# Operand places and a four-product last score tile in a fused attention and feed-forward block

## The reference

```python
xn = layernorm(x)                                   # no weights
q, k, v = (gelu(xn @ W1 + b1) @ W2 + b2 for each)   # 256 -> 256 -> 256
scores = tril(q @ k.T) / sqrt(256 * 512)            # a mask of zeros, no softmax
s = layernorm(scores @ v) * ln_w + ln_b
W = clip(round(W / (mean(abs(W)) + EPS)), -1, 1)    # for both feed-forward weights
g = silu(relu(xn @ W1q.T + b1) @ W2q.T + b2)        # 256 -> 1024 -> 256
out = x + s * g
```

## Time and profile before

| | before |
|---|---|
| median of 3 runs | 309.36 us (308.67 to 310.17) |
| the profiled execution | 308.97 us, its span 307.2 us |
| granted TensorE clock, mean | 0.998 of full speed |
| TensorE matmul busy | 301.1 us (98%) |
| VectorE busy | 246.6 us (80%) |
| ScalarE busy | 221.2 us (72%) |
| GpSimd busy | 134.6 us (44%) |
| chain that ended last | TensorE 89%, VectorE 4%, DMA 3% |

### The profile page before, as it was taken

How to read it: one execution, slowest core, us unless ns; L and a number is a source line. 1 busy time by engine, 2 the same in 40 slices (tenths; PEclk the granted TensorE clock), 3 DMA queues, 4 the chain that set the end, 5 groups by cost and what they waited for, 6 DMA issues and landing times.

```text
span 307.2 us, 5721 instructions
## 1 busy us (share of the span) xinstructions
PE 301.1 (98%) x1868; PEld 270.5 (88%) x1868; DVE 246.6 (80%) x540; ACT 221.2 (72%) x420; POOL 134.6 (44%) x104
## 2 busy tenths in 40 slices
PE   8999999999999999999999999999999999999994
PEld 8878899889988899888997889888998889988893
DVE  4889797967989588976989669895789858696686
ACT  3696948966786857949489576877579594795862
POOL 3945835168060942429151580608515292404100
PEclk9999999999999999999999999999999999999999
DMA  7960034420006000240005100060000500020001
GB/s 226 376 220 2 0 112 152 134 85 2 1 2 205 0 0 0 57 148 0 0 0 152 53 0 0 0 202 3 0 0 20 186 0 0 0 70 2 0 2 68
DMA packets 15228, 19.06 MB, mean 62 GB/s; under 512 B 1776, under 2 KB 12528, under 8 KB 15216
## 3 DMA queue, kind: packets, MB, share of 16 engines
q1 hardware_dynamic: 14656, 18.51, 18.9%
q10 hardware_dynamic: 560, 0.40, 0.4%
HBM read 14.69 MB, written 4.22 MB: 62 GB/s over the span
## 4 chain that ended last, share of the span: by engine, by line
PE 89%; DVE 4%; DMA 3%; SPq 1%; ACT 1%; issue 1%; POOL 0%; DVEq 0%
PE bank L830 89%; DMA x_all<-in_w1t 3%; DVE g_lo L642 1%; SPq L195 1%; DVE gw L748 1%; DVE gw L634 0%; DVE w1q L587 0%; DVE x_all L636 0%; ACT r_lo L398 0%; DVE gw L777 0%; PE bank L814 0%; SPq L206 0%; DVE s L585 0%; DVE y L754 0%; POOL o_rstd L357 0%
## 5 line engine op out<-in xcount | busy, mean ns | idle before, releaser
L724 DVE TENSOR_TENSOR r_lo<-bank,r_hi 128x512 fp32r<-128x512 f32 x64 | 44.0, 691 | 34.8 <-ACT bank L461 34.7
L460 ACT ACTIVATE r_hi<-bank,col 128x512 fp32r<-128x512 f32 x64 | 47.1, 735 | 24.0 <-PE bank L830 24.0
L357 POOL TENSOR_TENSOR o_rstd<-o_var,neg_half 128x2 f32<-128x2 f32 x16 | 11.2, 701 | 81.2 <-ACT o_var L484 81.2
L316 POOL TENSOR_TENSOR y<-y,xn 128x512 f32<-128x512 f32 x12 | 20.5, 1711 | 57.2 <-DMA y<-in_x_t 57.2
L461 ACT ACTIVATE bank<-bank,col 128x512 f32<-128x512 f32 x64 | 45.5, 711 | 0.0
L830 PE MATMUL bank<-xT_hi,w1q 128*128 128x512 f32 x128 | 39.7, 392 | 0.0
L830 PE MATMUL bank<-xT_lo,w1q 128*128 128x512 f32 x128 | 39.7, 392 | 0.0
L468 ACT CAST s_hi<-s 128x512 fp32r<-128x512 f32 (+3 forms) x32 | 14.7, 461 | 30.8 <-DVE s L712 28.0
L830 PE MATMUL bank<-w2q,r_lo 128*128 128x256 f32 x256 | 35.0, 279 | 0.0
L439 ACT ACTIVATE g_hi<-bank,col 128x512 fp32r<-128x512 f32 x48 | 34.0, 707 | 1.0 <-PE bank L830 0.9
L830 PE MATMUL bank<-w2q,r_hi 128*128 128x256 f32 x256 | 34.3, 276 | 0.0
(11 more groups left out here) (140 smaller groups left out, 700.7 us busy)
## 6 DMA issues: line engine op xcount, KB each, us to landing
out<-x_all SPq DMA_DIRECT2D x15, 256.0 KB, 3.1
x_all<-in_x SPq DMA_DIRECT2D x7, 512.0 KB, 3.6
xn<-x_norm_rows SPq DMA_DIRECT2D x6, 512.0 KB, 4.1
y<-in_x_t SPq DMA_DIRECT2D x6, 512.0 KB, 4.8
x_all<-in_w1t SPq DMA_DIRECT2D x2, 512.0 KB, 7.9
x_all<-in_w2t SPq DMA_DIRECT2D x1, 1024.0 KB, 10.4
row<-in_rows SPq DMA_DIRECT2D x1, 512.0 KB, 4.3
x_all<-in_x SPq DMA_DIRECT2D x1, 256.0 KB, 3.2
```

The source lines that it names most:

```text
L316: nc.gpsimd.tensor_tensor(half, half, x_mean_all, ALU.subtract).then_inc(xT_centred, 1)
L357: nc.gpsimd.tensor_tensor(o_rstd[:, half], o_var[:, half], neg_half[:, half], ALU.pow).then_inc(o_rstd_made, 1)
L460: nc.scalar.activation(r["hi"][:, f], pre[:], ACT.Relu, bias=b1)
L724: nc.vector.tensor_tensor(r["lo"][:, f], bank[(AT_F1 + f) % BANKS][:], r["hi"][:, f].bitcast(FP32), ALU.subtract).then_inc(r_split, 1)
```

## The change

Two things. First, declarations: W2v leaves `w` for tensors of its own (`w2v`), which stand with `w2q` ahead of `w`; `small` grows from 48 to 144 elements and moves in between, `gap` is new and unused, and `x_part` grows by what `small` took further down. By the same rounding, `w2v_hi`, `w2v_lo` and `w2q` then start at bytes 7520, 9568 and 11616, `w_hi`, `w_lo` and `w1q` at 20384, 28576 and 36768, and everything from `x_all` on starts 1024 bytes later than before, while `ones_r` stays. `g` becomes one tensor with hi and lo side by side, at the same distance as before. GpSimd's two instructions that make W2v's parts and the 24 matmuls of V name the new tensors.

Second, the last score tile (128 keys, 128 queries): instead of six matmuls of 128 columns there are four. z_hi is loaded once per k and multiplied with g_hi and g_lo side by side (256 columns), z_lo with g_hi (128 columns). The bank then holds hi\*hi + lo\*hi in columns 0 to 127 and hi\*lo in columns 128 to 255. ScalarE copies the second range to `s32` ahead of its four `s_hi` instructions, behind a wait for all four score tiles; VectorE adds the ranges and the key's bias in one instruction and applies the mask in a second.

```diff
-        w = {"hi": sb("w_hi", [P, 5, CK, C], FP32R), "lo": sb("w_lo", [P, 5, CK, C], FP32R)}
+        w2v = {"hi": sb("w2v_hi", [P, CK, C], FP32R), "lo": sb("w2v_lo", [P, CK, C], FP32R)}
+        w2q = sb("w2q", [P, FT, C], FP32R)
+        small = sb("small", [P, 144])
+        w = {"hi": sb("w_hi", [P, 4, CK, C], FP32R), "lo": sb("w_lo", [P, 4, CK, C], FP32R)}
         w1q = sb("w1q", [P, CK, F], FP32R)
-        w2q = sb("w2q", [P, FT, C], FP32R)
+        gap = sb("gap", [P, 112])
...
-        x_part = sb("x_part", [P, 4, TT])
+        x_part = sb("x_part", [P, 16, TT])
...
-        small = sb("small", [P, 48])
...
-        g = {"hi": sb("g_hi", [P, 6, T], FP32R), "lo": sb("g_lo", [P, 6, T], FP32R)}
+        g_both = sb("g", [P, 2, 6, T], FP32R)
+        g = {"hi": g_both[:, 0], "lo": g_both[:, 1]}
...
+                act.wait_ge(s_summed, 4 * i + 4)
+                if first:
+                    act.wait_ge(w2_quantized, 1)
+                else:
+                    act.wait_ge(s_split, 4 * i)
+                nc.scalar.copy(s32[:, S_AT[TT - 1]:S_AT[TT - 1] + P],
+                               bank[(AT_S + TT - 1) % BANKS][:, P:2 * P]).then_inc(s_part_copied, 1)
                 for j in range(TT):
                     act.wait_ge(s_read, 4 * i + j + 1)
...
+                    if j == TT - 1:
+                        at = slice(S_AT[j], S_AT[j] + P)
+                        dve.wait_ge(s_part_copied, i + 1)
+                        nc.vector.scalar_tensor_tensor(s32[:, at], src[:, 0:P], d[:, j:j + 1], s32[:, at],
+                                                       ALU.add, ALU.add).then_inc(s_part_made, 1)
+                        dve.wait_ge(s_part_made, i + 1)
+                        nc.vector.tensor_tensor(s32[:, at], s32[:, at], causal[:], ALU.mult).then_inc(s_read, 1)
+                        return
...
-                                             [(g[a][:, 4 + k, t * P:(t + 1) * P], w[b][:, 4, k])
+                                             [(g[a][:, 4 + k, t * P:(t + 1) * P], w2v[b][:, k])
...
-                for j in range(TT):
+                for j in range(TT - 1):
...
+                dst = claim(i, AT_S + TT - 1)
+                tail = slice(T - P, T)
+                both = [g_both[:, :, k, tail] for k in range(CK)]
+                sums = dst[:, 0:2 * P].rearrange("p (a t) -> p a t", a=2)
+                nc.tensor.matmul(sums, z["hi"][:, 0, tail], both[0], start=True, stop=False)
+                for k in range(CK):
+                    nc.tensor.matmul(dst[:, 0:P], z["lo"][:, k, tail], g["hi"][:, k, tail], start=False, stop=False)
+                nc.tensor.matmul(sums, z["hi"][:, 1, tail], both[1], start=False, stop=True).then_inc(s_summed, 1)
```

More of the change, by code:

```diff
@@ L166, in gated_block @@
         v_hi_made, v_split = sem("v_hi_made"), sem("v_split")
-        s_hi_made, s_split = sem("s_hi_made"), sem("s_split")
+        s_hi_made, s_split, s_part_copied, s_part_made = (
+            sem("s_hi_made"), sem("s_split"), sem("s_part_copied"), sem("s_part_made"))
         silu_made, s_made, s_gated = sem("silu_made"), sem("s_made"), sem("s_gated")
@@ L292, in _ @@
             pool.wait_ge(v_centred, CK)
-            nc.gpsimd.tensor_copy(w["hi"][:, 4], raw_qkv[:, 5]).then_inc(w2v_hi_made, 1)
+            nc.gpsimd.tensor_copy(w2v["hi"][:], raw_qkv[:, 5]).then_inc(w2v_hi_made, 1)
             pool.wait_ge(w2v_hi_made, 1)
-            nc.gpsimd.tensor_tensor(w["lo"][:, 4], raw_qkv[:, 5], w["hi"][:, 4].bitcast(FP32),
+            nc.gpsimd.tensor_tensor(w2v["lo"][:], raw_qkv[:, 5], w2v["hi"][:].bitcast(FP32),
                                     ALU.subtract).then_inc(w2v_split, 1)
```

## The result

The median went from 308.72 us (5 runs) to 307.08 (5 runs); the ratio is 0.9942, 95% interval 0.9928 to 0.9956: 0.6% faster, 1.6 us. The forecast was 1.2 us less. A time of 307 is also what half of the first rival (the waits give way) would have given, so the time alone doesn't tell the two apart; the traces do. The profiled execution is 307.08 us with a span of 305.3; against 308.97 and 307.2 that is 1.89 less.

What follows compares the result with a forecast made beforehand. TensorE, busy 98%, and its waits bound the kernel. Of 0.23 + 0.19 = 0.42 us per batch, r_lo's reserve passes 0.20; seven batches give 1.40, the end loses 0.20: 1.2 us less, from 309.36 to 308.2 us, range 306.5 to 310.0.

Steps and rivals of the forecast that it cites:

- the first rival: Stretches beside TensorE have more air or partly follow it: its whole 0.42 us per batch arrives, 306.2 us; half, 307; chance 0.20.
- What bounds: TensorE's pace, its waits at V and Y0, and the program's two ends; a batch gains 0.20 us.
- the wait at V: V's weight load is already 0.25 us late behind VectorE's last g_lo; the wait grows by 0.12 us.
- The reserve: At Y0, the load could go 0.20 us earlier before waiting for VectorE's last r_lo; this caps the batch's gain.
- Two weight loads: Last score tile, four products instead of six: two loads fewer save 0.23 us per batch, 0.15 as lower estimate.
- Places: Operands agreeing modulo 512 bytes in L1, Z and F1 save 2.4 ns per matmul, 0.19 us per batch.
- The end: Last batch: VectorE's second instruction, put at 0.35 us, delays the last s_hi and squares; 0.20 us lost.
- The rival with 0.15: A new wait at Y0 throws Y0, Y1, O and Y2 into 118 ns per matmul: slower, 311.9 us at worst; chance 0.15.
- The two rules: Trainium skill: by the isolated gap the four-product tile saves nothing; by independent read ports the places are worth 0.

## Why the prediction was right

- **What bounds.** Right in kind in both places, and the number is partly luck. V to V was put at 36.09 - 0.20 = 35.89 and is 35.88. What L1 and Z gained, 0.09 us, went into the wait at V, as forecast. At Y0 the load is held by r_lo, but it is 0.04 us late and not 0.1, and this takes only some 0.02 us. The reserve would have let 0.20 us through; TensorE itself gained 0.23 up to there and with the start of Y0 (the last tile 0.15, that start 0.06, F1 0.05, less 0.03 that S lost), where the prediction had 0.31. Sum and reserve came out nearly the same, so the cap hardly had to bind. That each wait is what it was taken for is shown by taking its cause away (V) or by making TensorE still faster ahead of it (Y0, where then all of the 0.05 us was waited away).
- **Two weight loads.** Put at 0.23 us per batch, with 0.15 as the lower bound. The tile itself gave 0.15, and the start of Y0 0.06 more where its load wasn't late (Y0 and Y1 5.52 to 5.46 us), 0.04 where it was: 0.21 and 0.19 in all. The term was near, though a part of it came behind the tile and not in it.
- **Places.** Put at 0.19 us, of which 0.08 in F1; measured are 0.05 in F1 and 0.09 in L1 and Z, 1.7 ns per matmul and not 2.4. The reason given was half of it: S left its 227 ns though its two operands had not moved against each other and lost 0.03 us, so one stage's pace was not proof for another's. L1's and Z's gain was waited away at V, as forecast.
- **The end.** Put at 0.20 us; 0.15 were lost. VectorE's instruction takes 0.29 us, 0.33 with its gap, as put (0.35). Of this 0.11 arrived at the end, where 0.20 was taken: the squares of O(0) and O(1) follow each other by 0.55 us without the instruction, as the second waits for O(1), and by 0.37 with it. So ScalarE had more idle time there than the prediction gave it, and the delay of s_hi went into that first. Some 0.05 more go, as far as is known, with V's slower pace, which no term had.
- **The slower pace behind a wait.** The rival with 0.15. In the changed kernel's trace Y and O don't show it. In the run with six products in the last batch it showed in Y and O of two batches, in the one without the mask in three, and over all kernels only where Y0's load was late. This fits the rival: the wait that the change brings to Y0 makes the slower pace possible, at some 0.35 us for each batch in which it happens. How often that is in the changed kernel isn't known from one trace, and what triggers it isn't shown.
- **The two rules.** The run with the tile alone is 0.34% faster; by the isolated gap of the Trainium skill (TensorE: Matmul & The Clock Gate, Back-to-back issue gap), columns over 2.4 plus 2.5 ns for each, it would have saved nothing. That section itself says that the isolated gap leaves out the weight loads and comes out too small for few columns, which the 103 ns of each narrow matmul here bear out. Other places moved F1 and L1 between 227 and 233 ns per matmul; the prediction took the Trainium skill's two independent read ports (the same page, Step-by-step: what each phase is for) to mean that places are worth nothing, and the runs show that they aren't.

Not settled: what in the state left behind by one stage picks 113 or 118 ns, and 227 or 231, for the next. In V, F1, L1 and S it happened without a wait too. Whether the places change how often it happens isn't shown. None of the twelve kernels is faster than the change beyond its interval.

## What to carry to other kernels

When the first engine is busy all the time, look for how much reserve the others have at each of its waits, in hundredths of a microsecond; a gain beyond that is waited away. Work out both the reserve and the sum of the gains; the smaller one gives the size of the result. Count narrow matmuls by their weight loads. Once no engine waits, the places of stationary and moving operands are worth one to three percent of each matmul of 512 columns, but try them as a set, since the pace of stages that were not touched changes with them. And when a change leaves a wait where there was none, look in several batches for a slower pace behind it.

## What the hardware showed that was not expected

- Matmuls of 512 fp32r columns with a new stationary operand each ran, in most batches, at 227 ns with both operands at the same place modulo 512 bytes or 256 apart, at 229 with 64 between, at 232 to 233 with 32 and 128. At the same place S ran at 231 after a D of 233 ns, and at 64 apart F1 ran at 233 in two batches. Of 256 columns they ran at 120 ns at the same place and at 113 or 118 with 64 bytes between.
- A stage can keep a slower pace to its end: 118 for 113 ns over all of Y and O in 13 of 51 batches in which Y0's first load was 0.02 to 0.10 us late, and in none of 53 in which it wasn't. V ran at 118 ns without a wait too.
- In the loop's batches a weight load that waited left 0.12 us after the end of the VectorE instruction that it waited for (r_lo at Y0, g_lo at V); at the first V of the program it left 0.05 us after it.
